# Grouping the second expert products with the state products, and one PSUM bank for reset gate and candidate

## The chip, the core and the metric

The kernel runs on one core of one Trainium2 chip. The metric is the time of one execution on the device in microseconds (us); of several runs the median is given. The core has a matrix engine (TensorE, "PE" in the profile; its weight loads are listed apart as "PEld"), a vector engine (VectorE, "DVE"), an activation engine (ScalarE, "ACT"), a general engine (GpSimd, "POOL") and SyncE ("SP"), which here only issues transfers. Each engine executes its own list of instructions in order. They meet at semaphores. PSUM, which TensorE writes, has eight banks; SBUF holds all else.

## The reference

`x` is [16, 256, 512]. A GRU with state size 512 runs over the 256 time steps for the 16 rows of the batch, starting from `cond`. Its states go through a mixture of eight low-rank experts, of which each token uses two, and the result is added to `x`.

```python
def cell(h, x):
    gi = x @ W_ih + b_ih
    gh = h @ W_hh + b_hh
    r = sigmoid(i_r + h_r); z = sigmoid(i_z + h_z)
    n = tanh(i_n + r * h_n)
    return (1.0 - z) * n + z * h
# over the states hs, as [4096, 512]:
norm = max(||hs||, 1e-12)
rw, sel = top_k(softmax(hs / norm @ router_w), 2); rw = rw / sum(rw)
combine = sum(one_hot(sel, 8) * rw[..., None], axis=1)
out = sum_e combine[:, e] * (hs @ Wa[e] @ Wb[e])      # Wa: 512x128, Wb: 128x512
return x + out
```

## The kernel before

**Numbers.** Every fp32 matrix is split into two fp16 parts, high and low, scaled by 128. A product of two such matrices is three matmuls (`TERMS`: high by high, high by low, low by high). Where two of them in a row use the same stationary operand, the second is issued without a weight load (`product(held, ...)`, `matmul_held`).

**Blocks and steps.** Time is cut into `NB` = 32 blocks of `S` = 8 steps; a block is 8 steps x 16 rows = 128 tokens. `n` counts the 256 steps, `i = n // 8` the blocks, and `s = n % 8` the step within its block. The 256 pairs of block and expert are numbered by `m`; expert `m % 8` of block `m // 8`.

**A step on TensorE.** `state_part(n)` multiplies the state with `W_hh`. It works in column groups: four products, each with a stationary operand of 32 columns, run beside each other in the four groups of 32 columns of the array and write the four groups of 32 PSUM partitions. Reset gate and candidate go to a bank `gates[n % 2]` (256 wide), the update gate to `zbank` (128 wide). Then `beside(n)` issues work that does not belong to the recurrence of this step: the first product of expert `m = n - DOWN` (`expert_down`, 12 matmuls of 128x128 to `ybank`), half of a part of the candidate's input product for the next block (`n_part`, 6 matmuls to `nbank`), the router when s = 3 (`route`, to other columns of `nbank`), the second product of expert `m = n - UP` (`expert_up`, 3 matmuls of 128x512 to `obank`), and half of the gates' input products for a later pair of steps (`pair_part`, 24 matmuls in column groups to `pairs`). The first three and `expert_up` use the whole array. `DOWN` is 8, `UP` and `ADD` are 13.

**The recurrence off TensorE.** On VectorE `gru_step(n)` transposes `gates` (L762), adds its high and low halves (L765), does the same with `zbank` (L768, L771), multiplies r by the candidate's part (L774), adds the input part (L779), forms z times the old state (L782), then u, the new state `st` in fp16 (L788) and in fp32 (L789), and the low part of the state (`high_low`, L746). Between these ScalarE computes r (L616), z (L620), 1-z (L622) and the tanh (L624). `copy_high` on ScalarE (L611) puts the high part beside the low one. TensorE's next `state_part` waits for `st` (`hhi_ready`) and, half-way, for both parts (`both_parts_ready`), and for its banks to hold the input products, which ScalarE copies there (`seed`, L578, one step ahead; `seed_z`, L588, right after the tanh).

**The rest of a step.** ScalarE reads the first product twice (`split_y`: high part of y at L658, y in fp32 at L662); the single buffer `y32` is free again when GpSimd has formed the low part from it (`low_y`, L458). ScalarE's `beside` also holds `read_router` (s = 3), `put_biases`, `add_gi_bias` (odd s, L606), `square` (s = 0), `gather_states` (s = 1 and 2, L638), `weigh` (s = 4, L653), and two reads of x (s = 5 and 7). GpSimd's `beside(n)` holds, in this order, sums of squares (s = 1, 2, 3: L440, L447, L451), `split_x` (s = 0 and 4, L433; it waits until both parts of the state of step n are there), `low_y`, `invert_norm` and `gaps` (s = 3), and `combine` (s = 4: L482, two of L486, L491), which makes the weights `comb` of the previous block. VectorE's `beside(n)`, after `gru_step(n)`, adds one weighted second product to the output, `add_expert(n - ADD)` (L815); for the first expert of a block it waits for all four operations of `combine`. At s = 3 `rank_experts` follows.

Of the kernel before, what the change touches and what calls it, by code (L numbers as in the profile page):

```python
# [9 lines left out]
ALU = mybir.AluOpType  # L10
# [18 lines left out]
def gru_moe_kernel(nc, x, cond, W_ih, W_hh, b_ih, b_hh, router_w, Wa, Wb, out):  # L29
# [7 lines left out]
    DOWN, UP, ADD = S, S + 5, S + 5  # L37
    YB = UP - DOWN + 1
# [11 lines left out]
    with ExitStack() as ctx:  # L50
# [93 lines left out]
        gates = [ps(f"gates{i}", [P, 4 * P]) for i in range(2)]  # L144
# [4 lines left out]
        ybank = ps("ybank", [P, 4 * P])  # L149
# [4 lines left out]
        LAST, LEFT = T - DOWN, T - UP  # L154
        last_y, last_o = [zbank, ybank], pairs + [obank] + gates


        first_banks = [obank, ybank, obank]

        def n_at(b, m):  # L160

            return (gates[1], zbank, nbank, obank)[m] if b == 0 else nbank

        def y_at(m):
            return ybank if m < LAST else last_y[(m - LAST) % 2]

        def o_at(m):
            return obank if m < LEFT else last_o[(m - LEFT) % len(last_o)]
# [35 lines left out]
        rh_summed = sem("rh_summed")  # L204
# [195 lines left out]
        def _(pool):  # L400
# [92 lines left out]
            def prepare_state():  # L493
# [4 lines left out]
                pool.wait_ge(primed, 3)  # L498
# [7 lines left out]
            def beside(n):  # L506
# [36 lines left out]
        def _(act):  # L543
# [26 lines left out]
            def seed(n):  # L570

                q = n % 2
                act.wait_ge(pair_done, n // 2 + 1)
                wait(act, rh_turned, n - 1)
                if n == 1:

                    act.wait_ge(gi_ready, 1)
                nc.scalar.activation(gates[n % 2][:, 0:2 * P], pairs[n // 2 % 2][:, 0:2 * P], ACT.Copy,  # L578
                                     scale=step_rows[:, q:q + 1]).then_inc(seeded, 1)
# [34 lines left out]
            def gru_step(n):  # L614
                act.wait_ge(rh_summed, n + 1)
# [48 lines left out]
            def beside(n):  # L664
# [15 lines left out]
                if s == 4 and 1 <= i:  # L680
                    weigh(i - 1)
# [41 lines left out]
            seed(1)  # L723
# [7 lines left out]
        def _(dve):  # L731
# [27 lines left out]
            def gru_step(n):  # L759
                g = gates[n % 2]  # L760
                dve.wait_ge(rh_done, n + 1)
                nc.vector.transpose(tr[:, 0:2 * K, :].rearrange("p (g k) c -> p g k c", k=K),  # L762
                                    g[:, 0:2 * P].rearrange("p (g c k) -> p g k c", g=2, k=K)).then_inc(rh_turned, 1)
                dve.wait_ge(rh_turned, n + 1)
                nc.vector.tensor_tensor(pre[:, 0:2, :, :].rearrange("p g k b -> p (g k) b"), tr[:, 0:2 * K, 0:B],  # L765
                                        tr[:, 0:2 * K, B:2 * B], ALU.add).then_inc(rh_summed, 1)
# [5 lines left out]
                                        ALU.add).then_inc(z_summed, 1)  # L772
                dve.wait_ge(r_ready, n + 1)
# [77 lines left out]
        def _(pe):  # L851
# [62 lines left out]
            def n_part(b, m, half):  # L914

                for i in range(6 * half, 6 * half + 6):
                    k, (pw, ph) = i // len(TERMS), TERMS[i % len(TERMS)]
                    if i == 0:
                        wait_turned(b)

                        pe.wait_ge(gi_ready, K * b + m)
                    if b >= 2 and m == 2 and i == 0:
# [4 lines left out]
                if half:  # L927
                    mm.then_inc(gi_done, 1)

            def first_parts(k):  # L930

                pe.wait_ge(weights_split, splits_before(3 * (k + 1)))
                for m in range(K):
                    for ph, pw in TERMS:

                        mm = nc.tensor.matmul(n_at(0, m)[:, 0:P], win[:, pw, k, m, :], turned(0, k, ph),
                                              start=(m >= 2 and k == 0 and (ph, pw) == TERMS[0]), stop=(k == K - 1),
# [5 lines left out]
            def first_state_part():  # L943
# [5 lines left out]
                sides = ((gates[0], slice(0, 2 * P), rh_done), (zbank, slice(2 * P, 3 * P), z_done))  # L949
# [14 lines left out]
            def state_part(n):  # L964
                g = gates[n % 2]
# [3 lines left out]
                for k in range(K):  # L969
                    for j in range(K):  # L970
                        nc.tensor.matmul(g[32 * j:32 * j + 32, 0:2 * P], st[:, k, :], whh[:, 1, k, j, 0:2 * P],  # L971
                                         start=False, stop=False, skip_group_check=True)
                pe.wait_ge(both_parts_ready, 2 * (n + 1))
                for k in range(K):
                    for j in range(K):
                        mm = nc.tensor.matmul(g[32 * j:32 * j + 32, 0:2 * P], prior[:, k, :], whh[:, 0, k, j, 0:2 * P],  # L976
                                              start=False, stop=(k == K - 1), skip_group_check=True)
                mm.then_inc(rh_done, 1)
                pe.wait_ge(z_seeded, n + 1)
                for k in range(K):  # L980
                    for j in range(K):
                        nc.tensor.matmul(zbank[32 * j:32 * j + 32, 0:P], st[:, k, :], whh[:, 1, k, j, 2 * P:3 * P],  # L982
                                         start=False, stop=False, skip_group_check=True)
                for k in range(K):
                    for j in range(K):
                        mm = nc.tensor.matmul(zbank[32 * j:32 * j + 32, 0:P], prior[:, k, :],  # L986
                                              whh[:, 0, k, j, 2 * P:3 * P], start=False, stop=(k == K - 1),
                                              skip_group_check=True)
                mm.then_inc(z_done, 1)

            def route(f):
# [3 lines left out]
                if f == NB - 2:  # L995
                    pe.wait_ge(gi_ready, K * NB)
# [15 lines left out]
            def expert_down(m):  # L1012
                f, e = m // NE, m % NE

                if m == LAST:
                    pe.wait_ge(z_turned, T)
                else:
                    wait(pe, yhi_ready, m if m <= LAST else m - 1)
                    wait(pe, y32_ready, m if m <= LAST else m - 1)
# [12 lines left out]
            def expert_up(m):  # L1032
                pe.wait_ge(ylo_ready, m + 1)
                if m < LEFT:
                    wait(pe, acc_done, m)
                elif o_at(m) is obank and m < LEFT + len(last_o):
                    pe.wait_ge(acc_done, LEFT)
                elif o_at(m) in pairs and m < LEFT + len(last_o):
# [3 lines left out]
                elif o_at(m) in gates and m < LEFT + len(last_o):  # L1042
                    pe.wait_ge(rh_turned, T)
                else:
                    pe.wait_ge(acc_done, m - len(last_o) + 1)
                if m in wb_split_at:
                    pe.wait_ge(weights_split, splits_before(wb_split_at[m]))
# [5 lines left out]
            def beside(n):  # L1053
                i, s = n // S, n % S
                if 0 <= n - DOWN < T:
                    expert_down(n - DOWN)
                if n == 1:
                    n_part(1, 0, 0)
                if 1 <= n and i + 1 < NB:
                    n_part(i + 1, s // 2, s % 2)  # L1060
                if s == 3 and 1 <= i:
                    route(i - 1)
                if 0 <= n - UP < T:
                    expert_up(n - UP)
                if n + AHEAD < T:
                    pair_part((n + AHEAD) // 2, (2, 3) if (n + 1) % 2 else (0, 1))
# [3 lines left out]
            def last_experts():  # L1070
# [3 lines left out]
                for m in range(LAST, T):  # L1074
                    expert_down(m)
                    expert_up(m + LEFT + 2 - LAST)
                    if m == LAST + 1:
                        route(NB - 1)
                for m in range(T + LEFT + 2 - LAST, T):
# [5 lines left out]
            for g, n_cols in ((gates[0], 2), (gates[1], 2), (zbank, 1)):  # L1085
# [13 lines left out]
            beside(0)  # L1099
            for n in range(1, T):  # L1100
                state_part(n)
                beside(n)
# [23 lines left out]
```

## Time and profile before

| what | value |
|---|---|
| median of 3 runs | 1043.08 us (1042.6 to 1044.17) |
| the profiled execution | 1042.75 us |
| its span (first to last instruction) | 1040.9 us |
| PE busy | 1010.8 us, 97% of the span |
| DVE busy | 860.1 us, 83% |
| ACT busy | 721.6 us, 69% |
| POOL busy | 298.4 us, 29% |
| granted clock of PE, mean | 0.998 of full speed |

Busy is the time in which an engine has an instruction under way. The 256 steps take nearly all of the span; before them weights are loaded and split, and after them the last experts are computed.

### The profile page before, as it was taken

The page shows a single profiled execution, that of the slowest core. Times are in us where ns is not written, and L with a number is a line of the kernel's source. Part 1 is how long each engine was busy: PE and PEld are TensorE (multiplying, and loading weights), DVE is VectorE, ACT ScalarE, POOL GpSimd, SP SyncE. Part 2 cuts the span into 40 slices and gives each one's busy share as a digit, 9 for nine tenths or more (in the row PEclk, how much of TensorE's full clock was granted, in tenths as well). Part 3 has the DMA queues.
Part 4 walks back from the last instruction along what each step waited for, and adds up shares of the span by engine and source line. Part 5 has one row for each costly group of instructions (what it writes and reads, how often), then busy time and mean ns, then how long its engine had stood idle before and what let it go on. Part 6 is the DMA issues. An engine that isn't in the chain of part 4 may idle for free.

```text
span 1040.9 us, 63058 instructions
## 1 busy us (share of the span) xinstructions
PE 1010.8 (97%) x28409; PEld 765.2 (74%) x24457; DVE 860.1 (83%) x3215; ACT 721.6 (69%) x2824; POOL 298.4 (29%) x762
## 2 busy tenths in 40 slices
PE   5789999999999999999999999999999999999997
PEld 3577777777777777777777777777777777777764
DVE  6889888888888888888888888888888888888886
ACT  7687666767666767667767667667766767766663
POOL 2032232322233322233332233332233332223223
PEclk9999999999999999999999999999999999999999
DMA  8230111111111111111111111111111111110001
GB/s 293 87 93 17 30 32 29 29 27 29 29 32 29 29 27 29 29 31 30 29 27 28 30 32 31 27 30 27 28 32 32 26 30 27 28 32 19 9 9 32
DMA packets 49506, 38.98 MB, mean 37 GB/s; under 512 B 34676, under 2 KB 39112, under 8 KB 49224
## 3 DMA queue, kind: packets, MB, share of 16 engines
q1 hardware_dynamic: 48376, 31.41, 11.1%
q8 instruction: 210, 3.44, 1.4%
q10 hardware_dynamic: 848, 3.54, 1.0%
q14 instruction: 72, 0.59, 0.2%
HBM read 18.94 MB, written 8.39 MB: 26 GB/s over the span
## 4 chain that ended last, share of the span: by engine, by line
PE 91%; DVE 5%; ACT 2%; DMA 1%; issue 1%; POOL 0%; ACTq 0%; DVEq 0%; POOLq 0%
PE pairs L863 13%; PE ybank L863 13%; PE gates L971 11%; PE gates L976 10%; PE obank L863 10%; PE nbank L863 6%; PE ybank L854 5%; PE zbank L982 5%; PE zbank L986 5%; PE pairs L854 5%; PE obank L854 5%; PE nbank L854 3%; DVE tr L762 1%; DMA wih<-in_L_cond_W_ih 1%; DVE pre L765 1%
## 5 line engine op out<-in xcount | busy, mean ns | idle before, releaser
L863 PE MATMUL pairs<-wx,xs 128*32 128x256 f16 x4096 | 215.1, 275 | 0.0
L863 PE MATMUL ybank<-hparts,wa 128*128 128x128 f16 x2016 | 212.6, 221 | 0.0
L458 POOL TENSOR_TENSOR y<-y 128x128 f16<-128x128 f32 x256 | 111.3, 435 | 348.4 <-ACT y L658 190.2
L863 PEld LDWEIGHTS pairs<-wx,xs 128*32 128x32 f16 x4096 | 108.6, 96 | 137.6 <-issue 101.7
L863 PEld LDWEIGHTS ybank<-hparts,wa 128*128 128x128 f16 x2016 | 158.9, 97 | 37.6 <-issue 0.7
L863 PE MATMUL obank<-wb,y 128*128 128x512 f16 x492 | 186.5, 379 | 0.0
L854 PE MATMUL ybank<-hparts,wa 128*128 128x128 f16 x1008 | 181.9, 219 | 0.0
L762 DVE STREAM_TRANSPOSE tr<-gates 128x256 f32<-128x256 f32 x256 | 115.1, 450 | 72.1 <-PE gates L976 68.2
L616 ACT ACTIVATE rr<-pre 128x64 f32<-128x64 f32 x256 | 65.6, 256 | 156.2 <-DVE pre L765 155.9
L971 PE MATMUL gates<-whh,st 128*32 128x256 f16 x4080 | 156.0, 273 | 11.9 <-DVE st L788 11.4
L976 PE MATMUL gates<-whh,hparts 128*32 128x256 f16 x4080 | 155.9, 273 | 0.0
L854 PE MATMUL pairs<-wx,xs 128*32 128x256 f16 x2048 | 144.7, 273 | 0.0
L815 DVE SCALAR_TENSOR_TENSOR acc<-obank,comb,acc 128x512 f32<-128x512 f32 x184 | 137.1, 745 | 0.2
L863 PE MATMUL nbank<-xs,win 128*128 128x128 f16 x992 | 123.6, 220 | 0.0
L971 PEld LDWEIGHTS gates<-whh,st 128*32 128x32 f16 x4080 | 107.7, 97 | 20.4 <-issue 18.2
L611 ACT ACTIVATE hparts<-st 128x64 f16<-128x64 f16 x257 | 65.9, 256 | 81.9 <-DVE st L788 81.6
L578 ACT ACTIVATE gates<-pairs,step_rows 128x256 f32<-128x256 f32 x256 | 115.2, 450 | 0.3 <-PE pairs L863 0.3
L976 PEld LDWEIGHTS gates<-whh,hparts 128*32 128x32 f16 x4080 | 109.8, 97 | 1.8
L620 ACT ACTIVATE zz<-pre 128x64 f32<-128x64 f32 x256 | 65.6, 256 | 58.9 <-DVE pre L771 58.8
L986 PE MATMUL zbank<-whh,hparts 128*32 128x128 f16 x4080 | 101.5, 219 | 0.0
L982 PE MATMUL zbank<-whh,st 128*32 128x128 f16 x4080 | 101.5, 219 | 0.0
L854 PE MATMUL nbank<-xs,win 128*128 128x128 f16 x496 | 95.9, 219 | 0.0
(142 smaller groups left out, 1982.7 us busy)
## 6 DMA issues: line engine op xcount, KB each, us to landing
out<-outb SPq DMA_DIRECT2D x63, 128.0 KB
xin<-in_x SPq DMA_DIRECT2D x58, 128.0 KB
wih<-in_L_cond_W_ih ACTq DMA_DIRECT2D x4, 768.0 KB, 7.4
whh<-in_L_cond_W_hh SPq DMA_DIRECT2D x4, 768.0 KB, 11.7
wih<-in_L_ffn_Wb SPq DMA_DIRECT2D x8, 256.0 KB, 2.6
xs<-xh SPq DMA_TRANSPOSE x116, 3.0
wih<-in_L_ffn_Wa SPq DMA_DIRECT2D x4, 256.0 KB, 5.2
whh<-in_L_ffn_Wa SPq DMA_DIRECT2D x4, 256.0 KB, 3.2
```

Of the source, the lines that this page charges most:

```text
L458: nc.gpsimd.tensor_tensor(y[:, m % YB, 1, :], y32[:, :], y[:, m % YB, 0, :], ALU.subtract).then_inc(ylo_ready, 1)
L578: nc.scalar.activation(gates[n % 2][:, 0:2 * P], pairs[n // 2 % 2][:, 0:2 * P], ACT.Copy, scale=step_rows[:, q:q + 1]).then_inc(seeded, 1)
L611: nc.scalar.activation(hparts[:, past(n), :, n % S, 0:B], st[:, :, 0:B], ACT.Copy).then_inc(both_parts_ready, 1)
L616: nc.scalar.activation(rr[:, :], pre[:, RG, :, :].rearrange("p k b -> p (k b)"), ACT.Sigmoid, scale=1 / PROD_SCALE).then_inc(r_ready, 1)
L762: nc.vector.transpose(tr[:, 0:2 * K, :].rearrange("p (g k) c -> p g k c", k=K), g[:, 0:2 * P].rearrange("p (g c k) -> p g k c", g=2, k=K)) ...
L815: nc.vector.scalar_tensor_tensor(out=(outb if e == NE - 1 else acc)[:, :], in0=o_at(m)[:, :], scalar=comb[:, e:e + 1], in1=(xin[:, f % XIN ...
L854: return nc.tensor.add_instruction(mybir.InstMatmult(name=nc.get_next_instruction_name(), engine=mybir.EngineType.PE, start_tensor_calc=start,
L863: return nc.tensor.matmul(out, lhsT, rhs, start=start, stop=stop, skip_group_check=True)
L971: nc.tensor.matmul(g[32 * j:32 * j + 32, 0:2 * P], st[:, k, :], whh[:, 1, k, j, 0:2 * P], start=False, stop=False, skip_group_check=True)
L976: mm = nc.tensor.matmul(g[32 * j:32 * j + 32, 0:2 * P], prior[:, k, :], whh[:, 0, k, j, 0:2 * P], start=False, stop=(k == K - 1), skip_gro ...
L982: nc.tensor.matmul(zbank[32 * j:32 * j + 32, 0:P], st[:, k, :], whh[:, 1, k, j, 2 * P:3 * P], start=False, stop=False, skip_group_check=True)
L986: mm = nc.tensor.matmul(zbank[32 * j:32 * j + 32, 0:P], prior[:, k, :], whh[:, 0, k, j, 2 * P:3 * P], start=False, stop=(k == K - 1), skip ...
```

## The change

The steps take turns. In odd steps (`wide_step`) TensorE does whole-array work: two first products and a full part of the candidate's input product, with the router at s = 3. In even steps (`grouped_step`) it does a full pair of gate input products and two second products, all in column groups of 32; for this the second product is cut by tokens, so that each of its three terms is four matmuls with 32 stationary columns (`expert_up_by_tokens`). The update gate's products hold their weights between two terms. Reset gate and candidate now have one bank, `gates`, for all steps; so `seed(n + 1)` moves to behind the tanh of step n, before `seed_z(n + 1)`. The freed bank makes a second `ybank`; second products go to `nbank` and `obank` in turn. The sum of high and low halves is cut into two instructions, for reset gate and for candidate, with a wait of its own for the second. `weigh` moves from `beside(n)` at s = 4 into ScalarE's `gru_step`, behind the tanh. `split_y` and `low_y` run twice in odd steps and not in even ones. `DOWN` goes from 8 to 9, `UP` and `ADD` from 13 to 12.

```diff
-    DOWN, UP, ADD = S, S + 5, S + 5
-    YB = UP - DOWN + 1
+    DOWN, UP, ADD = S + 1, S + 4, S + 4
+    YB = 6
...
         def o_at(m):
-            return obank if m < LEFT else last_o[(m - LEFT) % len(last_o)]
+            return (nbank, obank)[m % 2] if m < LEFT else last_o[(m - LEFT) % len(last_o)]
...
 # GpSimd, beside(n)
                 if s in (0, 4) and 1 <= i and i + 2 < NB:
                     split_x(i + 2, s // 4, n)
-                if 0 <= n - DOWN:
+                if s % 2 and 0 <= n - DOWN:
                     low_y(n - DOWN)
+                    low_y(n - DOWN + 1)
...
 # ScalarE, gru_step(n) and beside(n)
             def gru_step(n):
-                act.wait_ge(rh_summed, n + 1)
+                act.wait_ge(r_summed, n + 1)
...
+                if n % S == 4 and n >= S:
+                    weigh(n // S - 1)
                 if n + 1 < T:
+                    seed(n + 1)
                     seed_z(n + 1)
...
-                if 0 <= n - DOWN:
+                if s % 2 and 0 <= n - DOWN:
                     split_y(n - DOWN)
-                if n + 2 < T:
-                    seed(n + 2)
+                    split_y(n - DOWN + 1)
...
-                if s == 4 and 1 <= i:
-                    weigh(i - 1)
...
 # VectorE, gru_step(n)
-                nc.vector.tensor_tensor(pre[:, 0:2, :, :].rearrange("p g k b -> p (g k) b"), tr[:, 0:2 * K, 0:B],
-                                        tr[:, 0:2 * K, B:2 * B], ALU.add).then_inc(rh_summed, 1)
+                nc.vector.tensor_tensor(pre[:, RG, :, :], tr[:, RG * K:(RG + 1) * K, 0:B],
+                                        tr[:, RG * K:(RG + 1) * K, B:2 * B], ALU.add).then_inc(r_summed, 1)
+                nc.vector.tensor_tensor(pre[:, HN, :, :], tr[:, HN * K:(HN + 1) * K, 0:B],
+                                        tr[:, HN * K:(HN + 1) * K, B:2 * B], ALU.add).then_inc(hn_summed, 1)
...
+                dve.wait_ge(hn_summed, n + 1)
                 dve.wait_ge(r_ready, n + 1)
...
 # TensorE
+            def expert_up_by_tokens(m, n):
+                i, s = (n - 1) // S, (n - 1) % S
+                pe.wait_ge(ylo_ready, m + 1)
+                wait_sum_bank(m)
+                if o_at(m) is nbank and i + 1 < NB:
+                    pe.wait_ge(gi_ready, K * (i + 1) + s // 2 + 1)
+                if o_at(m) is nbank and s == 3:
+                    pe.wait_ge(router_read, i)
...
+                for t, (ph, pw) in enumerate(TERMS):
+                    for g in range(4):
+                        rows = slice(32 * g, 32 * g + 32)
+                        mm = product((ph, pw) == (0, 1), o_at(m)[rows, :], y[:, m % YB, ph, rows], wb[:, pw, m % NE, :],
+                                     t == 0, t == 2, 32, 32 * g)
+                mm.then_inc(o_done, 1)
...
+            def wide_step(n):
+                i, s = n // S, n % S
+                if 0 <= n - DOWN:
+                    expert_down(n - DOWN)
+                if i + 1 < NB:
+                    n_part(i + 1, s // 2, n)
                 if s == 3 and 1 <= i:
-                    route(i - 1)
...
+                    route(i - 1, n)
+                if 0 <= n - DOWN:
+                    expert_down(n - DOWN + 1)
+
+            def grouped_step(n):
+                pair_ahead(n, (2, 3) if n == 0 else (0, 1, 2, 3))
+                if 0 <= n - UP:
+                    expert_up_by_tokens(n - UP, n)
+                    expert_up_by_tokens(n - UP + 1, n)
```

`combine` and the order of GpSimd's `beside` are otherwise as they were, and so is `add_expert`, now called with `n - 12`.

## Rows read from the trace of the kernel before

**Rows 1.** The page, busy time by engine, and the waits: engine, line, what for, total, times, longest.
```profile
PE 1010.8 (97%) x28409; PEld 765.2 (74%) x24457; DVE 860.1 (83%) x3215; ACT 721.6 (69%) x2824; POOL 298.4 (29%) x762
...
PE gates L971 <- DVE st L788: 11.4, 15, 1.4
```

**Rows 2.** The timeline, DVE's first transposition of steps 123, 124, 128 (start, duration).
```profile
506.04 0.45 DVE L762 STREAM_TRANSPOSE tr<-gates 128x256 f32<-128x256 f32 x1 [0.33 <-PE gates L976]
...
510.27 0.45 DVE L762 STREAM_TRANSPOSE tr<-gates 128x256 f32<-128x256 f32 x1
...
525.66 0.45 DVE L762 STREAM_TRANSPOSE tr<-gates 128x256 f32<-128x256 f32 x1 [0.33 <-PE gates L976]
```

**Rows 3.** The chain of waits over step 122: start, length, engine, tile, line.
```profile
502.14 0.22 PE zbank L982 x16
...
502.59 0.16 PE ybank L863
...
503.37 0.06 PE nbank L863
...
503.70 0.22 PE obank L863
...
504.35 0.22 PE pairs L863 x4
...
505.12 0.43 PE gates L971 x16
```

**Rows 4.** The timeline, first transpositions of steps 3 and 4, before any expert work.
```profile
38.66 0.45 DVE L762 STREAM_TRANSPOSE tr<-gates 128x256 f32<-128x256 f32 x1 [0.25 <-PE gates L976]
...
42.38 0.45 DVE L762 STREAM_TRANSPOSE tr<-gates 128x256 f32<-128x256 f32 x1 [0.25 <-PE gates L976]
```

**Rows 5.** The timeline of step 122: DVE's sums and state, ACT's copy of the state.
```profile
502.68 0.29 DVE L765 TENSOR_TENSOR pre<-tr 128x128 f32<-128x128 f32 x1
...
502.89 0.31 DVE L768 STREAM_TRANSPOSE tr<-zbank 128x128 f32<-128x128 f32 x1
...
503.38 0.22 DVE L774 TENSOR_TENSOR rhn<-rr,pre 128x64 f32<-128x64 f32 x1
...
504.43 0.23 DVE L788 TENSOR_TENSOR st<-u,v 128x64 f16<-128x64 f32 x1
...
504.57 0.22 DVE L789 TENSOR_TENSOR hist<-u,v 128x64 f32<-128x64 f32 x1
504.69 0.26 ACT L611 ACTIVATE hparts<-st 128x64 f16<-128x64 f16 x1 [0.32 <-DVE st L788]
```

**Rows 6.** The timeline after step 126: ACT's second read of y, POOL's low part.
```profile
520.78 0.27 ACT L662 ACTIVATE y<-ybank 128x128 f32<-128x128 f32 x1
...
521.17 0.43 POOL L458 TENSOR_TENSOR y<-y 128x128 f16<-128x128 f32 x1 [3.42 <-ACT y L662]
```

**Rows 7.** The timeline of step 123: a POOL operation and DVE's sum at once.
```profile
506.50 0.40 POOL L451 TENSOR_TENSOR sqs<-sqs 128x128 f32<-128x128 f32 x1
...
506.53 0.52 DVE L765 TENSOR_TENSOR pre<-tr 128x128 f32<-128x128 f32 x1
```

**Rows 8.** The timeline: ACT gathering states (after step 9), POOL's squares (after step 121).
```profile
64.68 0.65 ACT L638 ACTIVATE hf<-hparts 128x512 f16<-128x512 f16 x1
...
501.35 0.73 POOL L440 TENSOR_TENSOR sq<-sq 128x256 f32<-128x256 f32 x1 [2.69 <-DVE hparts L746]
```

**Rows 9.** The timeline: state and POOL of step 124, then weights and their first use in the tail.
```profile
512.51 0.22 DVE L788 TENSOR_TENSOR st<-u,v 128x64 f16<-128x64 f32 x1
...
513.30 0.68 POOL L433 TENSOR_TENSOR xh<-x,xh 128x256 f16<-128x256 f32 x1 [1.88 <-DVE hparts L746]
...
513.93 0.43 POOL L458 TENSOR_TENSOR y<-y 128x128 f16<-128x128 f32 x1
...
1028.54 0.24 POOL L482 TENSOR_SCALAR wts<-wt 128x2 f32<-128x2 f32 x1
...
1030.06 0.75 DVE L815 SCALAR_TENSOR_TENSOR acc<-pairs,comb,xin 128x512 f32<-128x512 f32 x1 [1.89 <-PE pairs L863]
```

More of the change, by code:

```diff
@@ L141, in gru_moe_kernel @@
         outb = sb("outb", [P, D])
-        gates = [ps(f"gates{i}", [P, 4 * P]) for i in range(2)]
+        gates = ps("gates", [P, 4 * P])
         zbank = ps("zbank", [P, 4 * P])
@@ L722, in _ @@
             split_first(1)
-            seed(1)
             for n in range(T):
@@ L912, in put_first_biases, with n_part @@
                 mm.then_inc(bias_done, 1)
-            def n_part(b, m, half):
-                for i in range(6 * half, 6 * half + 6):
+            def n_part(b, m, n):
+                for i in range(len(TERMS) * K):
                     k, (pw, ph) = i // len(TERMS), TERMS[i % len(TERMS)]
@@ L921, in n_part @@
                         pe.wait_ge(gi_ready, K * b + m)
+                        wait(pe, acc_done, n - UP)
                     if b >= 2 and m == 2 and i == 0:
@@ L926, in n_part @@
                                  i == 0, i == 11)
-                if half:
-                    mm.then_inc(gi_done, 1)
+                mm.then_inc(gi_done, 1)
             def first_parts(k):
@@ L980, in state_part, with route @@
                 for k in range(K):
[L981 to L988, printed above, removed]
+                    for pw in range(2):
+                        for j in range(K):
+                            mm = product(pw == 1, zbank[32 * j:32 * j + 32, 0:P], prior[:, k, :],
+                                         whh[:, pw, k, j, 2 * P:3 * P], False, pw == 1 and k == K - 1, 2 * B, 32 * j)
                 mm.then_inc(z_done, 1)
-            def route(f):
+            def route(f, n):
                 if f == 0:
                     pe.wait_ge(weights_split, splits_before(N_RW_SPLITS))
-                if f == NB - 2:
-                    pe.wait_ge(gi_ready, K * NB)
+                wait(pe, acc_done, n - UP)
                 wait(pe, router_read, f)
@@ L1013, in expert_down @@
                 f, e = m // NE, m % NE
[L1015 to L1019, printed above, removed]
+                wait(pe, yhi_ready, m - 1)
+                wait(pe, y32_ready, m - 1)
                 if e == 0:
@@ L1030, in expert_down, with wait_sum_bank @@
                 mm.then_inc(y_done, 1)
+            def wait_sum_bank(m):
+                if m - LEFT in FROM_PAIRS:
+                    pe.wait_ge(seeded, T)
+                    pe.wait_ge(z_seeded, T)
+                elif m - LEFT == FROM_OBANK:
+                    pe.wait_ge(acc_done, LEFT)
+                elif m - LEFT == FROM_GATES:
+                    pe.wait_ge(rh_turned, T)
+                elif m - LEFT == FROM_ZBANK:
+                    pe.wait_ge(z_turned, T)
+                elif m > LEFT:
+                    pe.wait_ge(acc_done, m - len(last_o) + 1)
+                else:
+                    wait(pe, acc_done, m - 1)
             def expert_up(m):
                 pe.wait_ge(ylo_ready, m + 1)
[L1034 to L1038, printed above, removed]
-                    pe.wait_ge(seeded, T)
-                    pe.wait_ge(z_seeded, T)
[L1042 to L1047, printed above, removed]
+                wait_sum_bank(m)
                 for n, (ph, pw) in enumerate(TERMS):
@@ L1075, in last_experts @@
                     expert_down(m)
-                    expert_up(m + LEFT + 2 - LAST)
+                    expert_up(m - 2)
                     if m == LAST + 1:
-                        route(NB - 1)
-                for m in range(T + LEFT + 2 - LAST, T):
+                        route(NB - 1, T - 1)
+                for m in range(T - 2, T):
                     expert_up(m)
@@ L1098, in _ @@
             first_state_part()
-            beside(0)
+            grouped_step(0)
             for n in range(1, T):
                 state_part(n)
-                beside(n)
+                if n % 2:
+                    wide_step(n)
+                else:
+                    grouped_step(n)
             last_experts()
```

57 lines of the change are left out of this document (26 added, 31 removed).

## The prediction, before the result was known

> **What bounds the kernel now.** The page comes first: TensorE is busy for 1010.8 of 1040.9 us, and in all the waits it waits only 15 times for the new state, 11.4 us in all [rows 1]. So TensorE sets the pace. Next the period: VectorE's first transposition starts 15.39 us apart over four steps, which is 3.85 a step, and 4.23 over the step with the router (s = 3), 0.38 more [rows 2]. A block of eight is 7 x 3.85 + 4.23 = 31.16. Then the chain of waits splits one period [rows 3]: update gate 0.45; first product 0.78 (12 matmuls, the first 0.16 instead of the 0.06 of the next ones); half of the input part 0.33; second product 0.65; half a pair 0.77; and 0.87, the rest of 3.85, for reset gate and candidate. Those are 32 group matmuls of 256 columns, 0.11 per four. Half a pair has 24 of the same form and should take 0.66, so it pays 0.11 as well. Both surcharges stand where TensorE goes from column groups to the whole array or back: two switches of 0.11 in each step.
>
> Last, how close the second limit is. In steps 3 and 4, before any expert work, the period is 3.72 [rows 4]: that is the chain through VectorE and ScalarE alone, from the transposition of one step to that of the next. TensorE's lead over it is only 0.13.
>
> **TensorE's work after the change.** An even step has no switch: 0.45 + 2 x 0.66 + 2 x 0.65 + 0.87 = 3.94. I take the second product by column groups as equally long, since group matmuls now run four at once (16 of 256 columns in 0.44) [rows 3]. An odd step has both switches: 0.45 + 0.11 + 3 x 0.67 + 0.11 + 0.87 = 3.55, and 3.93 at s = 3 [rows 2, 3]. That would be 4 x 3.94 + 3 x 3.55 + 3.93 = 30.34 a block, 0.8 less than now, if nothing else were late. Holding weights in the update gate takes away loads, which lie beside matmuls, and no columns: nothing.
>
> **The chain of the recurrence.** The sum over 128 elements holds VectorE for 0.21 before the next transposition; each of the two over 64 elements should hold it for 0.14, as the two sums of the state do [rows 5]. That is 0.07 to 0.08 more ahead of everything that follows, and the engine's own rate decides there (r comes earlier than it is taken). The second wait ahead of the product with r: from 0, if it is worked off behind the running sum, to 0.08 (as much as an added sum costs); I take 0. The chain becomes 3.80, so odd steps take 3.80 and not 3.55, except s = 3. The copy of input products into the single bank (`seed`) now stands between the tanh and the copy of the state on ScalarE. That engine sits idle 0.32 ahead of L611 [rows 5], so I charge nothing; without that cover it is 0.1.
>
> **Two reads of y in one step.** Let U be the start of the new fp16 state. The next transposition is at U + 1.49 where the chain decides (3.72 less 2.23, the state's start after its transposition), the first sum 0.48 behind it at U + 1.97 [rows 2, 4, 5]. ScalarE's fp32 read of y starts at U + 0.58 and GpSimd's low part 0.39 later, for 0.43 [rows 2, 5, 6]. There is one `y32`, so the second expert's read waits for that: U + 1.45, and its low part runs from U + 1.84 to 2.27, across the first sum. When such an operation had begun 0.03 ahead of this sum, the sum took 0.52 instead of 0.29 [rows 7], as if it had started 0.14 before the other's end. Here that gives 2.27 - 0.14 - 1.97 = 0.16, and the even steps s = 0 and 6 come to 3.96, about TensorE's 3.94. At s = 1 the squares stand ahead of both low parts on GpSimd, from U + 0.76 for 0.73 [rows 8]; the second fp32 read slips to U + 1.97, behind it are queued `add_gi_bias` (about 0.4 until the next operation) and the gathering of states (0.65, I take 0.55 until the next) [rows 8], and r of the following step starts at U + 2.92 and is there at 3.2. VectorE would take it 1.18 + 0.08 behind the transposition, U + 2.75 [rows 5]. So s = 2 takes 3.80 + 0.44 = 4.24.
>
> The Trainium skill ("SBUF — State Buffer", section "SBUF: two separate sides") says that a VectorE operation with two SBUF inputs and a GpSimd operation that reads SBUF exclude each other, and that the loser is blocked for the whole instruction of the other. By that rule the sum would be 0.30 late instead of 0.16, and the whole run about 13 us longer (0.14 x 3 steps x 31 blocks); rows 7 show a delay of less than the whole instruction, and I go by them.
>
> **The weights of the experts.** Here I see the main cost. VectorE adds the first expert of a block at s = 4 now (`ADD` = 12) and did so at s = 5, a whole period later; it waits there for the last operation of `combine`. `weigh` is earlier, but `combine` stands behind `split_x` on GpSimd, which waits for both parts of the state of that same step. `split_x` starts 0.79 after U [rows 9], the next operation 0.63 later; from the first operation of `combine` to the use of its result it is 1.52 in the tail, where nothing disturbs it [rows 9]. So the addition can start at U + 2.94. The addition is queued in front of the next transposition; it holds VectorE for 0.67 of its 0.75. The transposition is at U + 3.61 instead of U + 1.49: 2.12 of stall. With 0.10 for the colliding sum that step takes 3.80 + 0.10 + 2.12 = 6.02. TensorE runs ahead meanwhile through step 5, and then waits. In the last two blocks there is no `split_x`; the stall is 0.9. Bounds: 1.9 if the operations of `combine` pipeline better, 2.3 if `low_y` and the gaps of s = 3 hold it up.
>
> **Sum.** Steps 0 to 7 of a block: 3.96 + 3.80 + 4.24 + 3.93 + 6.02 + 3.80 + 3.96 + 3.80 = 33.51, against 31.16: 2.35 more. 29 such blocks (1 to 29): 68.2. Block 30 with the shorter stall: 1.1. Block 31: 2, by the same terms (it has no input part, so its other steps are chain-bound before and after). Steps 0 to 8: 9 x 0.08 = 0.7. Tail: one more pair of reads of y ahead of the squares on the way to the last weights, 0.9. Together 73; the profiled execution took 1042.75 (span 1040.9, and 1.85 around it), the median is 1043.08. 1042.75 + 73 = 1116.
>
> **Rivals.**
> Only the stall (17%): `r` and the sums keep clear of ScalarE's queue and GpSimd. Then s = 0, 2 and 6 take TensorE's 3.94, s = 4 takes 5.92, a block 33.07: 29 x 1.9 + 4 = 59, 1102 us. For it: the margins are tenths; against: the s = 1 queue is long.
> A dearer chain (19%): the second wait costs 0.08 in seven steps of eight, 17 us, 1133 us. For it: it stands on the recurrence itself. Against: the add at the end of a step has two waits already and is not in the way.
> TensorE keeps setting the pace (4%): the other side. Place: the first addition of each block, and the chain behind it. It decides if the weights are ready 2.1 us sooner than I work out; then a block is 4 x 3.94 + 3 x 3.80 + 3.93 = 31.09, about 1041 us. For it: `weigh` has been moved ahead, and 31.09 is less than 31.16. Against: the wait for the state ahead of `split_x` [rows 9].
> Weights in time, the rest as forecast (3%): a block of 31.43, 29 x 0.27 + 2: 1053 us.
> The change does not do what it says (2%): the groups of a second product of 512 columns run one after another. Then two of them take 5.2 instead of 1.3, 3.9 more in each even step, over 1500 us. Against: groups of 256 columns overlap [rows 3].
>
> **Numbers.** My forecast has 55%, most of it between 1107 and 1126. The range of 1098 to 1135 takes in the rival with only the stall and the one with a dearer chain. 0.2% is what a measurement of this kernel can tell from no change. Faster by more than that: 0.03; within it: 0.02 (both from the rival in which TensorE sets the pace); slower: 0.95.
>
> **What would show it.** In the timeline after: GpSimd's `comb` ending 2 us after the moment at which VectorE is ready for the addition of s = 4, VectorE idle ahead of it, and a period of about 6.0 there in every block; TensorE waiting for the state in odd steps, 3.80 apart; no first matmul of 0.16 in even steps; r about 0.45 late at s = 2; VectorE's first sum stretched in even steps. I am wrong if the period at s = 4 stays below 4.5, if the odd steps come down to 3.55, or if even steps exceed 4.2.

## The result and the profile after

The changed kernel takes 1137.67 us (median; 1137.01 to 1139.64), the one before 1042.96 us in the same session: the ratio is 1.0909, with a 95% interval of 1.089 to 1.0928. The direction was forecast, the size was not: 1116 was predicted, and 1137.67 lies above the range's end of 1135. The profiled execution took 1137.79 us for a span of 1136.0 us.

First the page of the kernel after: busy time by engine, as in [rows 1], and three lines of its waits.

```profile
PE 1008.7 (89%) x30603; PEld 750.2 (66%) x21839; DVE 891.0 (78%) x3471; ACT 714.6 (63%) x2824; POOL 300.0 (26%) x762
...
DVE acc L816 <- POOL comb L493: 79.5, 31, 3.1
PE gates L972 <- DVE st L789: 58.1, 134, 2.3
...
DVE rhn L775 <- ACT rr L616: 12.8, 31, 0.9
```

TensorE has the same work as before (1008.7 us against 1010.8) in a span 95 us longer, so the time went into waiting. VectorE waits 31 times, once per block, for `comb`, and TensorE waits 134 times for the new state, where it waited 15 times before.

Then the timeline of step 204 (s = 4). These rows answer to [rows 9].

```profile
898.35 0.43 DVE L760 STREAM_TRANSPOSE tr<-gates 128x256 f32<-128x256 f32 x1
...
900.53 0.29 ACT L656 ACTIVATE wt<-gap,rnorm 128x2 f32<-128x2 f32 x1
...
900.82 0.22 DVE L789 TENSOR_TENSOR st<-u,v 128x64 f16<-128x64 f32 x1
...
901.34 0.25 ACT L611 ACTIVATE hparts<-st 128x64 f16<-128x64 f16 x1
...
901.76 0.67 POOL L435 TENSOR_TENSOR xh<-x,xh 128x256 f16<-128x256 f32 x1 [1.18 <-ACT hparts L611]
...
902.52 0.24 POOL L484 TENSOR_SCALAR wts<-wt 128x2 f32<-128x2 f32 x1
...
902.87 0.80 POOL L488 TENSOR_SCALAR pick<-expert_no,top_no,wts 128x8 f32<-128x8 f32 x2
...
903.75 0.20 POOL L493 TENSOR_TENSOR comb<-pick 128x8 f32<-128x8 f32 x1
...
904.06 0.75 DVE L816 SCALAR_TENSOR_TENSOR acc<-nbank,comb,xin 128x512 f32<-128x512 f32 x1 [2.62 <-POOL comb L493]
904.73 0.44 DVE L760 STREAM_TRANSPOSE tr<-gates 128x256 f32<-128x256 f32 x1
```

The weight `wt` is ready at 900.82. GpSimd does not take it: it stands at `split_x` until ScalarE's copy of the state is there (901.59), runs that, and only then begins `combine` at 902.52. The addition starts at 904.06 after 2.62 us of idle VectorE, and the next transposition 0.67 behind it: a period of 6.38 us.

The two smaller losses, in the timeline of steps 200 and 202:

```profile
882.65 0.43 POOL L460 TENSOR_TENSOR y<-y 128x128 f16<-128x128 f32 x1 [0.44 <-issue]
...
882.76 0.41 DVE L763 TENSOR_TENSOR pre<-tr 128x64 f32<-128x64 f32 x1
...
890.53 0.28 ACT L665 ACTIVATE y<-ybank 128x128 f32<-128x128 f32 x1 [0.90 <-POOL y L460]
...
890.96 0.63 ACT L641 ACTIVATE hf<-hparts 128x512 f16<-128x512 f16 x1
...
891.48 0.25 ACT L616 ACTIVATE rr<-pre 128x64 f32<-128x64 f32 x1
...
891.83 0.23 DVE L775 TENSOR_TENSOR rhn<-rr,pre 128x64 f32<-128x64 f32 x1 [0.38 <-ACT rr L616]
```

The second low part of y lies across VectorE's first sum, which takes 0.41 instead of 0.22. In step 202 ScalarE's second fp32 read waits 0.90 for GpSimd, the gathering of states follows, and VectorE, which waits for r, is idle for 0.38 ahead of its product.

The periods, from one first transposition to the next, show all of it. Each is the usual value (the median over blocks 3 to 29) of its step in the block, and the last column is their sum; 31.16 a block is what [rows 2] give for the kernel before. A few steps are longer than the usual value of their s. Below, a step of 24 to 247 that is more than 0.1 over it is called irregular, and the sum of what such steps have over it is the irregular excess: 4.6 us in the changed kernel, nothing in the kernel before.

| kernel | s=0 | 1 | 2 | 3 | 4 | 5 | 6 | 7 | block |
|---|---|---|---|---|---|---|---|---|---|
| before | 3.85 | 3.85 | 3.85 | 4.23 | 3.85 | 3.85 | 3.85 | 3.85 | 31.16 |
| predicted | 3.96 | 3.80 | 4.24 | 3.93 | 6.02 | 3.80 | 3.96 | 3.80 | 33.51 |
| after | 4.03 | 3.78 | 4.29 | 3.97 | 6.39 | 3.77 | 3.96 | 3.78 | 33.97 |
| a_const | 4.03 | 3.78 | 4.29 | 3.96 | 3.98 | 3.82 | 3.96 | 3.78 | 31.60 |
| b_combine_first | 4.03 | 3.78 | 4.28 | 3.96 | 4.82 | 3.77 | 3.96 | 3.78 | 32.38 |
| c_two_y32 | 3.92 | 3.79 | 3.95 | 3.96 | 6.10 | 3.77 | 3.92 | 3.78 | 33.19 |
| d_one_sum | 3.96 | 3.71 | 4.21 | 3.93 | 6.40 | 3.71 | 3.93 | 3.71 | 33.56 |
| e_up14 | 4.02 | 3.78 | 4.28 | 3.95 | 3.97 | 3.81 | 3.96 | 3.78 | 31.55 |
| f_three_edits | 3.92 | 3.71 | 3.92 | 3.93 | 3.93 | 3.75 | 3.93 | 3.71 | 30.80 |
| g_whole_second | 4.15 | 3.71 | 4.15 | 3.93 | 4.15 | 3.72 | 4.15 | 3.71 | 31.67 |
| h_weigh_late | 4.03 | 3.78 | 4.28 | 3.95 | 6.22 | 3.77 | 3.96 | 3.78 | 33.77 |

### The profile page after: what moved, and what is told of

Its sections match the earlier page's. It is cut to its first block and busy times, and to the rows that moved or that the text cites. A ratio compares the mean times of both kernels' runs of the same rounds, so it can differ in the third digit from the quotient of the medians.

```text
span 1136.0 us, 63208 instructions
## 1 busy us (share of the span) xinstructions
PE 1008.7 (89%) x30603; PEld 750.2 (66%) x21839; DVE 891.0 (78%) x3471; ACT 714.6 (63%) x2824; POOL 300.0 (26%) x762
## 5 line engine op out<-in xcount | busy, mean ns | idle before, releaser
L864 PE MATMUL pairs<-wx,xs 128*32 128x256 f16 x4096 | 192.8, 273 | 0.5 <-issue 0.5
L864 PEld LDWEIGHTS ybank<-hparts,wa 128*128 128x128 f16 x2048 | 164.4, 98 | 34.4 <-issue 21.1
L972 PEld LDWEIGHTS gates<-whh,st 128*32 128x32 f16 x4080 | 93.3, 95 | 127.8 <-ACT gates L578 122.2
L855 PE MATMUL pairs<-wx,xs 128*32 128x256 f16 x2048 | 150.4, 273 | 0.0
L864 PE MATMUL zbank<-whh,hparts 128*32 128x128 f16 x4080 | 148.0, 219 | 0.0
L855 PE MATMUL zbank<-whh,hparts 128*32 128x128 f16 x4080 | 148.0, 219 | 0.0
L864 PEld LDWEIGHTS pairs<-wx,xs 128*32 128x32 f16 x4096 | 117.3, 97 | 46.4 <-issue 1.4
L864 PE MATMUL nbank<-xs,win 128*128 128x128 f16 x992 | 103.3, 219 | 45.8 <-DVE acc L816 45.8
L864 PEld LDWEIGHTS zbank<-whh,hparts 128*32 128x32 f16 x4080 | 118.0, 97 | 12.5
L864 PEld LDWEIGHTS nbank<-xs,win 128*128 128x128 f16 x992 | 80.9, 98 | 57.2 <-issue 50.8
L665 ACT ACTIVATE y<-ybank 128x128 f32<-128x128 f32 x256 | 70.4, 275 | 71.9 <-POOL y L460 71.9
L864 PE MATMUL obank<-wb,y 128*32 128x512 f16 (+1 forms) x980 | 99.9, 379 | 0.0
```

The costliest lines, as they stand in the source:

```text
L665: nc.scalar.activation(y32[:, :], y_at(m)[:, 0:P], ACT.Copy, scale=1 / PART_SCALE).then_inc(y32_ready, 1)
L855: return nc.tensor.add_instruction(mybir.InstMatmult(name=nc.get_next_instruction_name(), engine=mybir.EngineType.PE, start_tensor_calc=start,
L864: return nc.tensor.matmul(out, lhsT, rhs, start=start, stop=stop, skip_group_check=True)
L972: nc.tensor.matmul(gates[32 * j:32 * j + 32, 0:2 * P], st[:, k, :], whh[:, 1, k, j, 0:2 * P], start=False, stop=False, skip_group_check=True)
```

## The experiments

### a_const: constant weights, the stall alone

```diff
-                if e == 0:
-                    dve.wait_ge(comb_step, (f + 1) * COMB_STEPS)
-                   ... scalar=comb[:, e:e + 1]
+                   ... scalar=const_w[:, e:e + 1]     # a tile of ones, written once
```

> The changed kernel, but the sums take constant weights of 1 from a tile that is written once, so the addition of a block's first expert waits for no weights (the output is not weighted; the router and the weights are still computed). Theory (VectorE's wait for the weights at s = 4 is the main cost): the period at s = 4 falls from 6.38 to 3.94 to 4.05 us, the other steps stay, and with 29 x 2.35 + 2 x 0.9 us less the time is about 1068 us. Rival (TensorE's waits for the shared bank of second products, 46 us in the waits of the changed kernel, cost time by themselves): the period at s = 4 or 5 stays above 5 and the time above 1110 us.

Measured: 1063.26 us, ratio to the kernel before 1.0191 [1.0174, 1.0208]. This kernel leaves the weighting out. The period at s = 4 is 3.98 and no other usual period moved by more than 0.05. The stall was worth 74 of the 95 us (up to 1.6 of them belong to a stretch at a lower clock, see the part on why the prediction was wrong). TensorE's waits for the shared bank disappear here together with their cause, the late addition, so this run alone does not price them. The trace of the changed kernel does: 28 of its 29 such waits lie at s = 5, which takes 3.77 like the other odd steps.

### b_combine_first: why the weights are late

```diff
+                if s == 4 and 1 <= i:
+                    combine(i - 1)
                 if s in (0, 4) and 1 <= i and i + 2 < NB:
                     split_x(i + 2, s // 4, n)
```

> The changed kernel with GpSimd's combine ahead of split_x at s = 4. Theory (the weights are late because combine is queued behind an operation that waits for the state of the same step): combine begins as soon as weigh is done, 2.70 us after the transposition instead of 4.17, and the addition 1.54 later; the period at s = 4 becomes 4.9 us in all blocks, as it is already in the last two without split_x (4.83). 29 x 1.48 = 43 us less: 1095 us. Rival (the operations of combine themselves, or weigh, are what is late): the period at s = 4 stays above 6, the time above 1130 us.

Measured: 1091.59 us, ratio 1.0461 [1.0444, 1.0479]. The timeline of step 204:

```profile
862.81 0.30 ACT L656 ACTIVATE wt<-gap,rnorm 128x2 f32<-128x2 f32 x1
...
863.20 0.24 POOL L484 TENSOR_SCALAR wts<-wt 128x2 f32<-128x2 f32 x1 [0.34 <-ACT wt L656]
...
864.48 0.20 POOL L493 TENSOR_TENSOR comb<-pick 128x8 f32<-128x8 f32 x1
864.64 0.67 POOL L435 TENSOR_TENSOR xh<-x,xh 128x256 f16<-128x256 f32 x1
864.78 0.75 DVE L816 SCALAR_TENSOR_TENSOR acc<-nbank,comb,xin 128x512 f32<-128x512 f32 x1 [1.06 <-POOL comb L493]
```

The period at s = 4 is 4.82, where 4.9 was expected. GpSimd now takes the weight as soon as it is there, and the addition still waits 1.06: the order on GpSimd made 46 us of the loss. Of the 28 that are left above a_const, the way through `weigh` and `combine` makes 0.84 in each of 31 blocks, 26 us.

### c_two_y32: two buffers y32

```diff
-        y32 = sb("y32", [P, P])
+        y32 = sb("y32", [P, 2, P])
...
-                wait(act, ylo_ready, m)
+                wait(act, ylo_ready, m - 1)
```

> The changed kernel with two buffers y32 in turn, so ScalarE's second fp32 read of y does not wait for GpSimd's low part. Theory (two reads in one step through one buffer delay r at s = 2 and put a GpSimd operation across VectorE's first sum in even steps): s = 2 from 4.28 to about 3.97, s = 0 from 4.03 to 3.96, s = 4 down 0.1, s = 6 to TensorE's 3.94; 0.5 us a block and some 2 us in the blocks in which weights are split: 1120 us. Rival (even steps are TensorE's anyway, the wait is hidden): within 2 us of 1137.7.

Measured: 1108.13 us, ratio 1.0622 [1.0604, 1.0639], 30 us less than the changed kernel where 18 were expected. The rival is out. The periods at s = 0, 2 and 6 came as forecast to within 0.04 (3.92, 3.95, 3.92). More than expected went at s = 4, 0.29 instead of 0.1, which is 8 us instead of 3: the first sum is no longer stretched, so the state starts 2.31 after the transposition and not 2.47, and `split_x` starts 0.82 after the state and not 0.94. More went also in block 1, 35.11 instead of 38.56 (up to 1.6 of it is the lower clock of the changed kernel there), and the irregular excess was 1.5 instead of 4.6 us. The timeline of step 202:

```profile
865.85 0.28 ACT L661 ACTIVATE y<-ybank 128x128 f16<-128x128 f32 x1
...
866.01 0.29 ACT L665 ACTIVATE y<-ybank 128x128 f32<-128x128 f32 x1
...
866.41 0.66 ACT L641 ACTIVATE hf<-hparts 128x512 f16<-128x512 f16 x1
...
866.57 0.82 POOL L460 TENSOR_TENSOR y<-y 128x128 f16<-128x128 f32 x2
...
867.08 0.39 DVE L763 TENSOR_TENSOR pre<-tr 128x64 f32<-128x64 f32 x1
...
867.50 0.26 ACT L616 ACTIVATE rr<-pre 128x64 f32<-128x64 f32 x1 [0.43 <-DVE pre L763]
```

The reads of y are 0.16 apart and ScalarE waits for VectorE again, not the other way round. The sum still takes 0.39: GpSimd's two low parts, behind the squares, reach across it at s = 2.

### d_one_sum: one sum for reset gate and candidate

```diff
-                nc.vector.tensor_tensor(pre[:, RG, :, :], tr[:, RG * K:(RG + 1) * K, 0:B],
-                                        tr[:, RG * K:(RG + 1) * K, B:2 * B], ALU.add).then_inc(r_summed, 1)
-                nc.vector.tensor_tensor(pre[:, HN, :, :], tr[:, HN * K:(HN + 1) * K, 0:B],
-                                        tr[:, HN * K:(HN + 1) * K, B:2 * B], ALU.add).then_inc(hn_summed, 1)
+                nc.vector.tensor_tensor(pre[:, 0:2, :, :].rearrange("p g k b -> p (g k) b"), tr[:, 0:2 * K, 0:B],
+                                        tr[:, 0:2 * K, B:2 * B], ALU.add).then_inc(r_summed, 1)
...
-                dve.wait_ge(hn_summed, n + 1)
```

> The changed kernel with one sum over reset gate and candidate, as before the change, and without the second wait ahead of the product with r. Theory (the second sum takes 0.07 on the recurrence, the wait nothing): odd steps 3.71 instead of 3.78, s = 4 and s = 0 0.07 less, s = 2 as it is: about 0.3 us a block, 1128 us. Rival (the wait costs another 0.07): odd steps 3.64, which is below the 3.71 that the kernel before showed without expert work, 1119 us.

Measured: 1122.23 us, ratio 1.0753 [1.0735, 1.0771]. Odd steps are at 3.71, 0.07 below 3.78, which is what the theory put on the second sum. The wait beside it cost nothing: in step 201 the product with r starts 0.14 after the sum ahead of it, with the wait (changed kernel) as without it (d_one_sum). s = 4 did not get shorter (6.40), against the expectation: the state starts 2.37 after the transposition and not 2.47, but ScalarE's copy of it, on which `split_x` hangs, comes 3.02 after the transposition and not 2.99. `weigh` stands ahead of that copy and needs GpSimd's `gaps`, which end no earlier than before (2.13 for 2.11). The other periods, blocks 1 and 2 and the irregular excess (3.7 instead of 4.6) together gave 15 us instead of 10.

### f_three_edits: three edits at once

`UP` and `ADD` 14 with eight buffers of y and two of `comb`, two buffers y32, and one sum; nothing of the computation is left out. This is the version to which the first four point.

```diff
-    DOWN, UP, ADD = S + 1, S + 4, S + 4
+    DOWN, UP, ADD = S + 1, S + 6, S + 6
-        comb = sb("comb", [P, NE])
+        comb = sb("comb", [P, 2, NE])
...  # combine(f)
-                wait(pool, acc_done, f * NE)
+                wait(pool, acc_done, (f - 1) * NE)
```

> The changed kernel with three edits: second products and their sums two steps later (UP and ADD 14, eight buffers of y, two of comb), two buffers y32, and one sum over reset gate and candidate. Theory (the losses are the late weights, the single y32 and the second sum, each a wait that stands on the recurrence, and without them the saved switches show): even steps at TensorE's 3.92 to 3.95, s = 3 at 3.93, the other odd steps at 3.71, a block of about 30.85 against 31.16 before the change, and 1033 us. Rival (the new order of TensorE's work brings a loss of its own, such as the short stops in mid-stream seen in some even steps of the changed kernel): 1042 us or more.

Measured: 1035.83 us, ratio 0.9932 [0.9918, 0.9945]: faster than the kernel before by 0.7%. The periods came as expected, but for s = 5 (3.75 for 3.71). The missing 3 us against 1033 are in part irregular steps (1.7 us), and the stretch behind the last transposition is 1.2 us longer than in the kernel before; the second products come two steps later there.

### g_whole_second: the same with second products on the whole array

```diff
-                    for g in range(4):
-                        rows = slice(32 * g, 32 * g + 32)
-                        mm = product(..., o_at(m)[rows, :], y[:, m % YB, ph, rows], wb[:, pw, m % NE, :], ..., 32, 32 * g)
+                    mm = product(..., o_at(m)[:, :], y[:, m % YB, ph, :], wb[:, pw, m % NE, :], ...)
```

> The same kernel as f_three_edits, but the second products in even steps use the whole array, three matmuls of 128x512 each, so an even step has two switches between column groups and the whole array again. Theory (a switch costs 0.11, a second product by column groups costs what it costs on the whole array): even steps 0.22 longer, about 4.15, 27 us more than f_three_edits. Rival (the products by groups are themselves slower and eat what the switches give): the same time as f_three_edits within 3 us.

Measured: 1059.87 us, ratio 1.016 [1.0145, 1.0176], 24 us above f_three_edits. The chain of waits of both kernels over the second products of an even step, f_three_edits first:

```profile
824.51 0.11 PE pairs L861 x4
824.62 0.21 PE nbank L861 x4
824.84 0.22 PE nbank L852 x4
...
825.49 0.22 PE obank L852 x4
825.70 0.22 PE obank L861 x4
825.92 0.44 PE gates L969 x16
```

```profile
826.43 0.11 PE pairs L861 x4
826.54 0.32 PE nbank L861
826.86 0.22 PE nbank L852
...
827.51 0.22 PE obank L852
827.72 0.22 PE obank L861
827.94 0.55 PE gates L969 x16
```

Four group matmuls of 512 columns take 0.22, as one on the whole array does. What differs is the entry into the whole array (0.32 for 0.21) and the way back (0.55 for 0.44): the two switches of 0.11, and the even periods are 4.15 against 3.92.

### e_up14: later second products alone

The three lines shown for f_three_edits, with eight buffers of y, on the changed kernel.

> The changed kernel with second products and sums two steps later alone (UP and ADD 14, eight buffers of y, two of comb); nothing is left out of the computation. Theory (the stall is only the order of combine against the first sum of a block): s = 4 falls to 3.98 as with constant weights, no other step rises, about 1064 us. Rival (the late products collide with something else, or the combine of s = 4 now delays GpSimd's other work): a new long step elsewhere, over 1080 us.

Measured: 1064.81 us, ratio 1.0209 [1.0193, 1.0224]. With true weights the stall is gone as with constant ones (3.97 at s = 4), and no other usual period rose, but for s = 5 (3.81 for 3.77). The stretch behind the last transposition is 1.3 us longer.

### h_weigh_late: weigh behind the copy of the state

```diff
 # ScalarE, gru_step(n)
-                if n % S == 4 and n >= S:
-                    weigh(n // S - 1)
 # ScalarE, beside(n)
+                if s == 4 and 1 <= i:
+                    weigh(i - 1)
```

> The changed kernel with weigh put back behind the copy of the state at s = 4, ahead of the rest of ScalarE's other work. Theory (weigh ahead of the input copies delays the copy of the state by 0.15 to 0.2, GpSimd's split_x waits for both parts of the state, and combine stands behind it): the period at s = 4 gets shorter, from 6.38 to 6.2, about 5 us in all, 1132 us. Rival (combine needs weigh early): the period gets longer, over 6.5, 1141 us or more.

Measured: 1131.55 us, ratio 1.0852 [1.0835, 1.0868]; s = 4 at 6.22, which over 29 blocks is 5 of the 6 us. The timeline of step 204:

```profile
893.57 0.23 DVE L789 TENSOR_TENSOR st<-u,v 128x64 f16<-128x64 f32 x1
...
893.83 0.26 ACT L611 ACTIVATE hparts<-st 128x64 f16<-128x64 f16 x1
893.99 0.28 ACT L654 ACTIVATE wt<-gap,rnorm 128x2 f32<-128x2 f32 x1
...
894.36 0.67 POOL L435 TENSOR_TENSOR xh<-x,xh 128x256 f16<-128x256 f32 x1 [1.04 <-DVE hparts L745]
...
895.12 0.24 POOL L484 TENSOR_SCALAR wts<-wt 128x2 f32<-128x2 f32 x1
```

The copy follows the state by 0.26 instead of 0.52, and `split_x` begins 0.79 after the state, the distance that [rows 9] show, instead of 0.94. Moving `weigh` ahead, which was to bring the weights earlier, made them later, because the order on GpSimd hangs on the copy. In the last two blocks, which have no `split_x`, it does help: there s = 4 takes 5.47 with the late `weigh` and 4.83 with the early one.

### i_more_loads: more weight loads

```diff
-                            mm = product(pw == 1, zbank[...], prior[:, k, :], whh[:, pw, k, j, 2 * P:3 * P], ...)
+                            mm = product(False, zbank[...], prior[:, k, :], whh[:, pw, k, j, 2 * P:3 * P], ...)
```

> The kernel f_three_edits with the update gate's weights loaded again for its second term: 16 more weight loads a step, some 4,080 more instructions on TensorE, the same matmuls. Theory (the short stops in mid-stream come where TensorE's instructions are densest, since they are gone with whole-array second products, which have 2,178 matmuls and 1,452 loads less): more or longer stops, the excess over the usual periods in steps 24 to 247 rises from 1.7 us to over 5 us, usual periods unchanged, 1040 us. Rival (the loads lie beside matmuls and the stops have another cause): the same within 1.5 us of 1035.8.

Measured: 1042.87 us (1040.93 to 1046.55), ratio 0.9998 [0.9987, 1.0009]: 7 us more than f_three_edits, with the same usual periods and an excess of 6.5 us in steps 24 to 247. The timeline of its step 76, the longest of them:

```profile
323.41 0.38 PE L861 MATMUL pairs<-wx,xs 128*32 128x256 f16 x5
...
324.86 0.29 PE L861 MATMUL pairs<-wx,xs 128*32 128x256 f16 x3 [1.07 <-issue]
```

TensorE stops for over a microsecond within one run of matmuls, at a granted clock of 1.00, and waits for nothing that the profile shows.

## Why the prediction was wrong

The mechanism was right and sizes were off, the largest in the stall for the experts' weights. The forecast's block was 33.51 us, the measured one 33.97. Of the 22 us between 1115.75 and the profiled 1137.79:

- **The weights of the experts**, the main term, is the step that failed: 6.02 was predicted at s = 4, 6.39 is the usual value, 0.37 x 29 = 11 us. `split_x` was put 0.79 after the state; it came 0.94 after it. I had worked out that `weigh` is earlier, but not that on ScalarE it is now ahead of the copy of the state, and that GpSimd's `split_x` waits for this very copy; I had called the new order of ScalarE free on the strength of 0.32 of idle time [rows 5], without `weigh` in it. h_weigh_late measures it: 0.16. Then `combine` began 0.76 after `split_x` and not 0.63: I had taken the distance from a `low_y` behind it, an operation of another kind [rows 9]. The 1.52 (1.54 measured) and the 0.67 were right. (The row of the tail from which 1.52 was read puts the addition's wait down to TensorE [rows 9]; `comb` ended there at 1029.97, 0.09 ahead of the addition, so it was what came last.) The rest is the state's own start, 2.47 after the transposition instead of 2.41.
- **Blocks 1 and 2**: I gave them the same addition as all others. Block 1 took 38.56 and not 34.0 (31.65 before, plus 2.35). There ScalarE also splits weights; at s = 2 this stands behind the second read of y, the gathering included, so r comes at 2.22 after the transposition and the period is 5.87. With two buffers it is 4.12. Beyond the terms above blocks 1 and 2 have some 5 us. Not all of it is ScalarE's order. In the profiled execution TensorE idles 2.30 at s = 2 of block 1, waiting for the state, and then the granted clock falls from 1.00 to 0.50, from 2.4 to 1.2 GHz, for 3.4 us. h_weigh_late, with the same program for TensorE, has r as late and the same idle time, but its clock stays. First the changed kernel, then h_weigh_late; each time the wait, and the stretch behind it with the busy times of the engines, the granted clock, the share of the DMA engines and their GB/s:

```profile
69.10 0.97 PE L972 MATMUL gates<-whh,st 128*32 128x256 f16 x16 [2.30 <-DVE st L789]
...
69.20:72.60 3.40, 3.40 (x73) 2.72 (x51) 2.28 (x9) 1.82 (x7) 1.57 (x3) 0.50 0.43 109
```

```profile
69.67 0.62 PE L972 MATMUL gates<-whh,st 128*32 128x256 f16 x16 [2.30 <-DVE st L789]
...
69.80:73.20 3.40, 3.40 (x110) 3.08 (x72) 2.84 (x12) 2.68 (x10) 1.66 (x3) 1.00 0.44 114
```

h_weigh_late takes 5.11 in that step and 3.93 in the next, the changed kernel 5.87 and 4.77. So the queue on ScalarE makes 1.0 of the step (5.11 for 4.12), and the half clock 1.6 over both. b_combine_first, d_one_sum and e_up14 show such a stretch too, a_const and c_two_y32 do not. Why the clock falls in some and not in others stays open.

- **The irregular steps**: 4.6 us that the prediction had no term for. They belong to the change: the kernel before has none, g_whole_second 0.2, f_three_edits 1.7, i_more_loads 6.5. More weight loads at the same matmuls bring more of them. By what mechanism an engine stops was not found; that it is the supply of instructions is argued from the idle time put down to issue, not shown.
- **s = 0**: 4.03 for 3.96. The additional wait of that step (for `gi_n`) costs 0.07 on the recurrence: in step 200 VectorE adds the input part 0.32 after the product with r, in step 201 it is 0.25. `gi_n` itself is not late: it is there 0.50 after the transposition, 1.25 ahead of that addition. The trace before had it hidden under TensorE, and I left it out. 2 us.

Point by point, what held. Two switches of 0.11 a step before, none in an even step after: shown by g_whole_second, where they come back. Even steps at 3.94 of TensorE's work: 3.92 in f_three_edits, where nothing else is late. The chain at 3.80: 3.78, and 3.71 with one sum, so the second sum costs 0.07 (the second wait nothing, see d_one_sum). The single y32: 4.24 predicted at s = 2, 4.29 measured. The collision of GpSimd and VectorE: predicted 0.16, and the sum took 0.19 longer (0.41 for 0.22).

The Trainium skill ("SBUF — State Buffer", section "SBUF: two separate sides") has the loser blocked for the whole instruction of the other. Step 200 shows less than that: GpSimd's operation ends at 883.08, the sum had been issued at 882.76, 0.32 earlier, and lost 0.19. The times of GpSimd are rough in this profile, so the difference of 0.13 is not sharp; that the sum took 0.19 longer is.

Of the rivals, TensorE keeping the pace would have needed the weights 2.1 us earlier; e_up14 grants that and more and still takes 1064.81, so that rival was short of two further losses. "Weights in time, the rest as forecast", 1053, is the case of a_const and e_up14 and came 10 us low for the same reasons as the forecast, but for the stall.

## What to carry to other kernels

When work is moved to an earlier step, follow each of its producers to the step in which it is made and list what stands ahead of it in its engine's order; here one operation that waited for the newest state stood ahead of small ones whose input was there, and cost 46 us. Moving one producer ahead helps only if it passes nothing that the others wait for. And a saving on the engine that sets the pace counts only down to the next chain: by the sum of its rows TensorE's work fell by 0.8 us a block, and 0.36 is what shows of it once the three new losses are taken out.

## What the hardware showed that was not expected

Short stops. With second products in column groups, TensorE at times stops within a run of matmuls for 0.1 to over 1 us, at a granted clock of 1.00 in those steps. The kernel before had 28,409 matmuls and 24,457 loads and no irregular step; g_whole_second, with 28,407 and 20,375, had one; f_three_edits, with 30,585 and 21,827, had eight; i_more_loads, with 30,585 and 25,907, had seventeen, and its time scatters over 5.6 us. The total of instructions does not explain it (f_three_edits has fewer than the kernel before), their density within even steps may.

TensorE is not the only engine that stops. The one irregular step of g_whole_second, step 59, shows no stop on TensorE. VectorE pauses there ahead of an addition and waits for nothing that the profile shows, as it does in step 59 of f_three_edits:

```profile
261.98 0.75 DVE L813 SCALAR_TENSOR_TENSOR acc<-obank,comb,acc 128x512 f32<-128x512 f32 x1 [0.22 <-issue]
```

In the changed kernel step 27 has such a pause on VectorE, and at step 68 GpSimd is the one that pauses. An account by the density of TensorE's instructions does not cover these.

Nor are the places random. Steps 46, 96, 134, 168, 190, 206 and 226 are irregular in the changed kernel, in b_combine_first and in h_weigh_late alike; these have the same program for TensorE, and in step 134 it stops ahead of the same matmul in all three. But a_const has that program too, and none of the seven is irregular there. So the place in the program matters and does not decide alone.
